# Layer-norm scaling as one VectorE operation per 128 rows, and new orders of work, in a macaron block of FFN, windowed attention and FFN

## The reference

```
def _layernorm(x, axis=-1, eps=1e-05):
    m = jnp.mean(x, axis=axis, keepdims=True)
    v = jnp.var(x, axis=axis, keepdims=True)
    return (x - m) / jnp.sqrt(v + eps)

x = x + 0.5 * ffn(_layernorm(x)); x = x + attn(_layernorm(x)); x = x + 0.5 * ffn(_layernorm(x))
```

```
shared = silu(X @ sW1 + sb1) @ sW2 + sb2
logits = einsum('btd,ed->bte', X, routing_W) + expert_bias
activation = sqrt(softplus(logits)); top_vals, top_idx = top_k(activation, 2)
routed = sum over e of combine[e] * (silu(X @ rW1[e] + rb1[e]) @ rW2[e] + rb2[e])
```

## Time and profile before

| quantity | value |
|---|---|
| median of 3 runs | 1796.23 us |
| the profiled execution | 1796.92 us |
| span of its instructions | 1795.2 us |
| PE busy | 1611.3 us (90%) |
| DVE busy | 1398.3 us (78%) |
| ACT busy | 1255.8 us (70%) |
| POOL busy | 991.3 us (55%) |
| PE's mean granted clock | 0.967 of full speed |

### The profile page before, as it was taken

One profiled execution on the slowest core, in us unless ns is written; L12 is line 12 of the kernel. 1 busy time (PEld: TensorE's weight loads), 2 busy tenths in 40 slices (PEclk: granted clock), 3 DMA queues, 4 the chain that ended last, 5 costly groups with the idle time before them and its releaser, 6 DMA issues.

```text
span 1795.2 us, 35300 instructions
## 1 busy us (share of the span) xinstructions
PE 1611.3 (90%) x10304; PEld 1412.1 (79%) x10304; DVE 1398.3 (78%) x4802; ACT 1255.8 (70%) x3656; POOL 991.3 (55%) x917
## 2 busy tenths in 40 slices
PE   1679899999999999999999999999999999998866
PEld 1557788888887888888787888888888888877755
DVE  4457688888879888888888888887988888785733
ACT  2247678687777768787777867787776868776732
POOL 1434465655566566656666565566656665653524
PEclk9979999999999999999999999999999999999878
DMA  3134443545453453535344353535345453534201
GB/s 90 55 113 115 130 122 108 143 121 145 123 143 92 122 150 114 144 115 153 112 123 123 108 144 117 149 121 144 97 114 156 113 143 116 157 96 133 75 24 59
DMA packets 286420, 211.94 MB, mean 118 GB/s; under 512 B 162666, under 2 KB 240900, under 8 KB 286228
## 3 DMA queue, kind: packets, MB, share of 16 engines
q1 hardware_dynamic: 282736, 209.57, 40.9%
q10 hardware_dynamic: 3460, 0.04, 0.1%
q0 software_dynamic: 32, 0.07, 0.0%
HBM read 146.06 MB, written 42.47 MB: 105 GB/s over the span
## 4 chain that ended last, share of the span: by engine, by line
PE 42%; DVE 19%; POOL 13%; issue 12%; ACT 9%; DMA 3%; SPq 3%; POOLq 0%; DVEq 0%; ACTq 0%
POOL zz L400 6%; PE gb L773 5%; PE gb L775 5%; PE gb L774 5%; PE yb L773 4%; PE yb L775 4%; PE yb L774 4%; PE ptb L832 3%; POOL gl L406 3%; PE sb_ L823 3%; POOL pr L384 2%; ACT xn L493 2%; DVE ag L725 2%; ACT pr L465 2%; DVE cfs L697 2%
## 5 line engine op out<-in xcount | busy, mean ns | idle before, releaser
L406 POOL TENSOR_TENSOR gl<-ag,gh 128x512 fp32r<-128x512 f32 x288 | 376.0, 1312 | 200.6 <-ACT gh L519 188.6
L384 POOL TENSOR_TENSOR pr<-pr,rinv 128x512 f32<-128x512 f32 x256 | 281.0, 1098 | 300.1 <-DVE rinv L667 299.9
L465 ACT ACTIVATE pr<-pr,mx 128x128 f32<-128x128 f32 x1024 | 397.0, 396 | 56.2 <-DVE mx L659 56.1
L773 PE MATMUL yb<-w2h,gh 128*128 128x256 f32 x1152 | 333.4, 289 | 6.2 <-POOL gl L406 6.2
L774 PE MATMUL yb<-w2h,gl 128*128 128x256 f32 x1152 | 322.2, 280 | 0.0
L775 PE MATMUL yb<-w2l,gh 128*128 128x256 f32 x1152 | 321.8, 279 | 0.0
L400 POOL TENSOR_TENSOR zz<-lp,phalf 128x8 f32<-128x8 f32 x128 | 220.0, 1734 | 117.1 <-DVE lp L622 117.1
L471 ACT ACTIVATE pth<-ptb 128x512 fp32r<-128x512 f32 x256 | 151.4, 591 | 173.8 <-PE cxb L775 95.0
L719 DVE SCALAR_TENSOR_TENSOR ag<-gb,b,gate 128x512 f32<-128x512 f32 x256 | 190.5, 744 | 92.1 <-ACT tt L525 66.7
L725 DVE SCALAR_TENSOR_TENSOR ag<-tt,ag 128x512 f32<-128x512 f32 x288 | 249.6, 867 | 3.1
L659 DVE CUSTOM_DVE_ANT_0 pr<-sb_,mask 128x128 f32<-128x128 f32 x1024 | 236.1, 286 | 14.6 <-issue 11.6
(11 more groups left out here) (144 smaller groups left out, 3577.9 us busy)
## 6 DMA issues: line engine op xcount, KB each, us to landing
gate<-gates_pair SPq DMA_DIRECT2D x256, 256.0 KB, 3.8
ks<-qk_dram SPq DMA_DIRECT2D x256, 128.0 KB, 3.0
qs<-qk_dram SPq DMA_DIRECT2D x512, 64.0 KB, 2.9
qk_dram<-qkh SPq DMA_DIRECT2D x64, 256.0 KB, 3.9
qk_dram<-qkl SPq DMA_DIRECT2D x64, 256.0 KB, 3.8
vb<-va SPq DMA_DIRECT2D x32, 384.0 KB, 6.8
xres<-L_attn_x_dram SPq DMA_DIRECT2D x16, 512.0 KB, 4.3
cx<-cd SPq DMA_DIRECT2D x512, 16.0 KB, 1.8
```

Of the source, the lines that this page charges most:

```text
L384: nc.gpsimd.tensor_tensor(pr[:, k], pr[:, k], rinv[:, k, :].unsqueeze(2).to_broadcast([P, NP, P]), ALU.mult).then_inc(a_pn, 1)
L406: nc.gpsimd.tensor_tensor(gl[:, k, :], ag[:, k, :], gh[:, k, :].bitcast(F32), ALU.subtract).then_inc(f_gl, 1)
L465: nc.scalar.activation(pr[:, k, r, :], pr[:, k, r, :], ACT.Exp, bias=mx[:, k, r:r + 1], scale=-1.0, accum_out=rsum[:, k, r:r + 1]).then_in ...
L773: nc.tensor.matmul(dst, ah, bh, start=start, stop=False, **kw)
```

## The change

The normalised rows are no longer made on ScalarE as x * rs + nb, but on VectorE as (x - mean) * rs, one `tensor_scalar` of 128x256 with two values per row. The four instructions of each `N2` step move from ScalarE to VectorE. GpSimd no longer computes nb, so `rstd` has two instructions where it had four, and the constant `mone` goes. The five orders are new, and the steps begin at another point of the pipeline.

```
-            def rstd(vals, r, neg, s, done):
+            def rstd(vals, r, s, done):
                 nc.gpsimd.tensor_tensor(r, vals[:, :, 1], epsb[:], ALU.add).then_inc(s, 1)
-                nc.gpsimd.tensor_tensor(neg, vals[:, :, 0], mone[:], ALU.mult).then_inc(s, 1)
-                pool.wait_ge(s, done + 2)
+                pool.wait_ge(s, done + 1)
                 nc.gpsimd.tensor_tensor(r, r, mhalf[:], ALU.pow).then_inc(s, 1)
-                pool.wait_ge(s, done + 3)
-                nc.gpsimd.tensor_tensor(neg, neg, r, ALU.mult).then_inc(s, 1)
...
-                    for t in range(NT):
-                        nc.scalar.activation(xn[:, t, :], src[:, t, :], ACT.Identity, bias=nb[:, t:t + 1],
-                                             scale=rs[:, t:t + 1]).then_inc(f_xn, 1)
...
+                elif s[1:] == "N2":
+                    n = nth(s, b)
+                    dve.wait_ge(f_rstd, 2 * n + 2)
+                    wait(dve, f_g1, 16 * n)
+                    wait(dve, a_xt, 2 * b if s[0] == "p" else 2 * min(b + 2, B))
+                    src = xin if s[0] == "p" else x2
+                    for t in range(NT):
+                        nc.vector.tensor_scalar(xn[:, t, :], src[:, t, :], mv[:, t, 0:1], rs[:, t:t + 1],
+                                                ALU.subtract, ALU.mult).then_inc(f_xn, 1)
```

`aN2` changes in the same way, with `mva` and `rsa`. Of the orders, one line of ScalarE's list (it shows `pt0` ahead of `pcr`, and no `N2`):

```
-cd14-1 pt0+1 ex1+0 cd15-1 pt1+1 ph0+0 qgh8-2 pct+1 pgh0+1 vh1+0 ex2+0 cd0+0 cth1-1 ph1+0 pt2+1 pgh1+1 ex3+0
+cd13-1 qgh7-2 pt0+1 pcr+1 ph15-1 cd14-1 ex0+0 pct+1 cd15-1 qgh8-2 ex1+0 pgh0+1 ph0+0 pt1+1 vh1+0 ex2+0 pt2+1
```

More of the change, by code:

```diff
@@ L19 @@
 ORDER_PE = """
[L20 to L24, removed]
@@ L25 @@
-S15+0 P13+0 qH8-1 qY5-1
+qH8-2 qY5-2 U13-1 P14-1 pH0+1 S0+0 pC+1 U14-1 P15-1 qY6-2 S1+0 pH1+1 U15-1 qY7-2 S2+0 P0+0 V1+0 qY8-2 pH2+1 U0+0
+P1+0 S3+0 pH3+1 pY0+1 S4+0 O0-1 O1-1 pH4+1 P2+0 U1+0 pY1+1 pH5+1 pY2+1 U2+0 qX0-1 qX1-1 S5+0 P3+0 pH6+1 qL-1
+pY3+1 pY4+1 S6+0 P4+0 U3+0 pH7+1 pH8+1 S7+0 P5+0 pY5+1 U4+0 pY6+1 qH0-1 S8+0 U5+0 qC-1 P6+0 pY7+1 pY8+1 qH1-1
+S9+0 U6+0 P7+0 qH2-1 S10+0 qY0-1 U7+0 P8+0 aX0+1 qH3-1 aX1+1 S11+0 qY1-1 U8+0 P9+0 Q00+1 qY2-1 Q01+1 U9+0 P10+0
+pX0+2 S12+0 pX1+2 qH4-1 qH5-1 pL+2 S13+0 P11+0 U10+0 qH6-1 Q10+1 Q11+1 qY3-1 S14+0 P12+0 U11+0 qH7-1 qY4-1 U12+0
@@ L26 @@
+P13+0 S15+0 V0+1
 """
 ORDER_ACT = """
-cd14-1 pt0+1 ex1+0 cd15-1 pt1+1 ph0+0 qgh8-2 pct+1 pgh0+1 vh1+0 ex2+0 cd0+0 cth1-1 ph1+0 pt2+1 pgh1+1 ex3+0
[L29 to L32, removed]
@@ L33 @@
-qgh4-1 ex13+0 qgh5-1 ph12+0 cd11+0 qh11+1 qt6-1 ex14+0 qt7-1 qgh6-1 cd12+0 ph13+0 vh0+1 ex15+0 qt8-1 ph14+0
-cd13+0 qgh7-1 pcr+2 ex0+1 ph15+0
+cth0-1 qt6-2 ex13-1 qh11+0 cd11-1 ph12-1 qgh5-2 ex14-1 cd12-1 qt7-2 vh0+0 ph13-1 qgh6-2 ex15-1 qt8-2 ph14-1
+cd13-1 qgh7-2 pt0+1 pcr+1 ph15-1 cd14-1 ex0+0 pct+1 cd15-1 qgh8-2 ex1+0 pgh0+1 ph0+0 pt1+1 vh1+0 ex2+0 pt2+1
+ph1+0 cth1-1 pgh1+1 pt3+1 ex3+0 cd0+0 pgh2+1 ph2+0 pt4+1 pgh3+1 cd1+0 pt5+1 ex4+0 cd2+0 qxh0-1 qxh1-1 pgh4+1
+ph3+0 pt6+1 ex5+0 pgh5+1 qen-1 pgh6+1 ph4+0 cd3+0 pt7+1 ex6+0 pt8+1 pgh7+1 cd4+0 ph5+0 pgh8+1 ex7+0 qt0-1 qcr-1
@@ L35 @@
+ph6+0 cd5+0 ex8+0 qgh0-1 qt1-1 qct-1 ph7+0 cd6+0 ex9+0 qt2-1 qgh1-1 ph8+0 cd7+0 axh0+1 axh1+1 qt3-1 qgh2-1
+ex10+0 cd8+0 qh00+1 ph9+0 ex11+0 qh01+1 pxh0+2 ph10+0 pxh1+2 cd9+0 qgh3-1 qt4-1 ex12+0 qt5-1 ph11+0 pen+2 cd10+0
+qgh4-1 qh10+1
 """
 ORDER_DVE = """
-ri15-1 mx0+0 pl14-1 qa8-2 mx1+0 ri0+0 pl15-1 pa0+1 qg8-2 ri1+0 pg0+1 mx2+0 pl0+0 vl1+0 pa1+1 pg1+1 qT-2 mx3+0
-pl1+0 pa2+1 ri2+0 pg2+1 aR0-1 pa3+1 aR1-1 qN1-1 ri3+0 pg3+1 pl2+0 mx4+0 pa4+1 pa5+1 pg4+1 qxl0-1 qxl1-1 mx5+0
-pg5+1 ri4+0 pl3+0 qLr-1 ri5+0 qLq-1 qR1-1 mx6+0 pl4+0 pa6+1 pg6+1 mx7+0 pa7+1 pl5+0 pg7+1 ri6+0 pa8+1 pg8+1
@@ L40 @@
[L40 to L43, removed]
+ri0+0 mx1+0 pa0+1 pg0+1 ri1+0 mx2+0 pl0+0 vl1+0 pa1+1 ri2+0 qT-2 pg1+1 pl1+0 mx3+0 pa2+1 pg2+1 pa3+1 aR0-1 pg3+1
+aR1-1 ri3+0 qN1-1 mx4+0 pl2+0 pa4+1 qN2-1 pg4+1 pa5+1 ri4+0 pg5+1 qxl0-1 qxl1-1 mx5+0 pl3+0 pa6+1 qLr-1 pg6+1
@@ L44 @@
+ri5+0 qLq-1 qR1-1 mx6+0 pl4+0 pa7+1 pg7+1 ri6+0 pa8+1 mx7+0 pg8+1 pl5+0 qR2-1 qa0-1 mx8+0 qg0-1 pl6+0 ri7+0 pT+1
+ri8+0 aN1+1 mx9+0 pl7+0 qa1-1 aN2+1 qg1-1 ri9+0 qa2-1 mx10+0 qg2-1 pl8+0 axl0+1 axl1+1 pN1+2 qa3-1 ri10+0 mx11+0
+pl9+0 pN2+2 ql00+1 ql01+1 qg3-1 ri11+0 pxl0+2 pxl1+2 mx12+0 pl10+0 qa4-1 qg4-1 ri12+0 pLr+2 qa5-1 pLq+2 mx13+0
+pl11+0 pR1+2 qa6-1 ri13+0 mx14+0 qg5-1 pl12+0 qg6-1 ql10+1 ql11+1 ri14+0 mx15+0 vl0+1 pl13+0 qa7-1 qg7-1 ri15+0
+pR2+2 pl14+0 mx0+1 qa8-1 pl15+0 qg8-1
 """
 ORDER_POOL = """
-pn11-1 qgl3-2 ctl0-1 pn12-1 qgl4-2 qgl5-2 pzz0+1 pn13-1 pzz1+1 pn14-1 pzz2+1 pzz3+1 qgl6-2 pn15-1 qgl7-2 pn0+0
@@ L47 @@
-pn1+0 qgl8-2 pgl0+1 ctl1-1 pgl1+1 pn2+0 pgl2+1 qrs-1 pn3+0 pgl3+1 pn4+0 pn5+0 pgl4+1 pgl5+1 qzz0-1 qzz1-1 qzz2-1
-pgl6+1 qzz3-1 pn6+0 pgl7+1 pgl8+1 pn7+0 qgl0-1 rsa+1 pn8+0 qgl1-1 prs+2 pn9+0 qgl2-1 pn10+0
+pn0+0 qgl8-2 pn1+0 pgl0+1 ctl0-1 ctl1-1 pgl1+1 pn2+0 pgl2+1 pn3+0 qrs-1 pgl3+1 pgl4+1 pn4+0 pgl5+1 pn5+0 pgl6+1
+qzz0-1 qzz1-1 qzz2-1 qzz3-1 pn6+0 pgl7+1 pgl8+1 pn7+0 qgl0-1 pn8+0 rsa+1 qgl1-1 pn9+0 qgl2-1 prs+2 pn10+0 pn11+0
+qgl3-1 pn12+0 qgl4-1 pzz0+2 pn13+0 pzz1+2 pzz2+2 qgl5-1 pzz3+2 pn14+0 pn15+0 qgl6-1 qgl7-1
@@ L350, in select @@
                 pool.wait_ge(w_const, done)
[L351 to L361, removed]
+            select(ident[:], ALU.not_equal, 1.0, 0, [[-1, P]], 1, 8)
+            select(mask[0:WIN, 0, :], ALU.is_ge, NEG, 0, [[-1, P]], 1, 9)
+            select(mask[0:WIN, 1, :], ALU.is_ge, NEG, -1, [[1, P]], -1, 10)
+            select(mask[0:WIN, 1, :], ALU.is_ge, NEG, WIN, [[-1, P]], 1, 11)
+            select(before[:], ALU.is_gt, 0.0, 0, [[1, E], [-1, E]], 0, 12)
+            select(rowlo[:, 0:1], ALU.is_ge, 0.0, -48, [[0, 1]], 1, 13)
+            select(rowlo[:, 0:1], ALU.is_ge, 0.0, 57, [[0, 1]], -1, 14)
+            select(rowlo[:, 0:1], ALU.not_equal, 0.0, -56, [[0, 1]], 1, 15)
             pool.dma_start(mask[WIN:2 * WIN, :, :], mask[0:WIN, :, :]).then_inc(w_mask, 16)
             pool.wait_ge(w_mask, 16)
-            def rstd(vals, r, neg, s, done):
+            def rstd(vals, r, s, done):
                 nc.gpsimd.tensor_tensor(r, vals[:, :, 1], epsb[:], ALU.add).then_inc(s, 1)
-                nc.gpsimd.tensor_tensor(neg, vals[:, :, 0], mone[:], ALU.mult).then_inc(s, 1)
-                pool.wait_ge(s, done + 2)
+                pool.wait_ge(s, done + 1)
                 nc.gpsimd.tensor_tensor(r, r, mhalf[:], ALU.pow).then_inc(s, 1)
-                pool.wait_ge(s, done + 3)
-                nc.gpsimd.tensor_tensor(neg, neg, r, ALU.mult).then_inc(s, 1)
             def step(s, b):
@@ L434, in step @@
             def step(s, b):
-                if s == "aN2":
-                    act.wait_ge(a_rstd, 4 * b + 4)
-                    act.wait_ge(f_g1, 16 * max(2 * b, 1))
-                    for t in range(NT):
-                        nc.scalar.activation(xn[:, t, :], x1[b % 2][:, t, :], ACT.Identity, bias=nba[:, t:t + 1],
-                                             scale=rsa[:, t:t + 1]).then_inc(a_xn, 1)
-                elif s[:3] == "axh":
+                if s[:3] == "axh":
                     c = int(s[3])
@@ L626, in step @@
                     dve.wait_ge(f_res, 2 * nth("p", b) + 2)
-                    wait(dve, a_rstd, 4 * b)
+                    wait(dve, a_rstd, 2 * b)
                     stats(x1[b % 2], stata, mva, a_stat, 8 * b)
+                elif s == "aN2":
+                    dve.wait_ge(a_rstd, 2 * b + 2)
+                    dve.wait_ge(f_g1, 16 * max(2 * b, 1))
+                    for t in range(NT):
+                        nc.vector.tensor_scalar(xn[:, t, :], x1[b % 2][:, t, :], mva[:, t, 0:1], rsa[:, t:t + 1],
+                                                ALU.subtract, ALU.mult).then_inc(a_xn, 1)
                 elif s[:3] == "axl":
@@ L679, in step @@
                         dve.wait_ge(a_x2, 2 * b + 2)
-                    wait(dve, f_rstd, 4 * n)
+                    wait(dve, f_rstd, 2 * n)
                     stats(xin if s[0] == "p" else x2, stat, mv, f_stat, 8 * n)
+                elif s[1:] == "N2":
[4 more added lines that the diff above has]
+                    src = xin if s[0] == "p" else x2
+                    for t in range(NT):
+                        nc.vector.tensor_scalar(xn[:, t, :], src[:, t, :], mv[:, t, 0:1], rs[:, t:t + 1],
+                                                ALU.subtract, ALU.mult).then_inc(f_xn, 1)
                 elif s[1:3] == "xl":
@@ L743, in _ @@
         def _(pe):
-            pe.wait_ge(w_const, 16)
+            pe.wait_ge(w_const, 15)
             pe.wait_ge(w_lo, NSPLIT + 2)
```

26 lines of the change are left out of this document (9 added, 17 removed).

## The result

The changed kernel takes 1806.73 us (median of 7 runs, 1803.74 to 1809.76) against 1796.23 us (7 runs, 1793.80 to 1799.24). The ratio is 1.0057, with a 95% interval of 1.0046 to 1.0069. It is slower by 10 us where 26 us faster was forecast. The profiled execution took 1807.23 us with a span of 1805.2 us.

The account below looks back on a forecast made before the run. TensorE's matmul stream was taken as the bound; 14 x (-1.0 router's chain, -0.6 small waits) = -22.4, ends -4, together -26 us on 1796.9, giving 1770 us; range 1735 to 1810, the forecast case's own 1760 to 1784.

Parts of the forecast that it names:

- small waits: PE's short waits before `S1`, `qX0` and `pX0`: expected to shrink by 0.6 us an iteration (0 to 0.64).
- The router's chain: Second FFN's router, from first logit instruction on DVE to `qC` on PE: 18.7 instead of 19.67 us, -1.0 an iteration.
- The powers: Four powers on POOL in the second FFN's router: 6.45 us instead of 8.13, as `pgl6` leaves them.
- no row says that a stall goes: Reason for taking only -1.0 us in the router; with the stalls of L606, L697 and L704 gone, -3.7.
- a stall or two leaves the router's chain: Rival: one DVE stall less per iteration gives 13 us more, two 25; 1745 to 1757 us, chance 0.18.
- PE's two waits: PE's waits before `S7` and `qC`, behind the second FFN's router: from 4.2 to 3.2 us an iteration.
- DVE's scalings: Twelve new `tensor_scalar` per iteration on DVE: 0.53 us each, 6.4 us in all (4.2 to 9.3), put at 0 cost.
- the stall of L605: DVE, router's ranks: 0.423 us, called the most a group shows on average; upper bound of one scaling 0.354 + 0.423.
- DVE's load: DVE's work per iteration: from 87.6 to 94.0 us (91.8 to 96.9), below the 102.5 us period, so covered.
- The slow rival: Throughout the loop DVE becomes the bound: 104.3 us an iteration, +21 us, 1817 us; chance 0.18.
- The ends: First transposes, batch 0's attention norm, last FFN's norm: each 1.1 us shorter, 3.3, plus 0.7 for start order; -4 us.
- The rule on what excludes what: On DVE and POOL: `tensor_scalar` and a GpSimd instruction can exclude each other, putting DVE's sum between middle and upper value.

## Why the prediction was wrong

**The step that failed is one that the prediction does not have.** Its sum counts DVE, ACT, POOL and PE, part by part, and nothing for SyncE. The other moves of the new orders went in as "small waits", -0.6 us. `OUT-2` behind `VS+0` stands in the diff of the lists, and the wait of `aR0` for the store is in the trace of before, at 3.2 us in 11 iterations. One such wait, 1.05 us, even stands in the row that gave the length of an iteration. The question to put to it was how far the store can be late. The answer was there: the store landed at 732.4 (728.77 + 3.6), 0.4 us before DVE was ready for `aR0` and 0.9 before it started at 733.27. In other iterations it took up to 5.1 us and `aR0` already waited. So nearly every microsecond more was going to hold DVE. Put right, this one word turns 1806.7 into 1770.9.

**How 3.84 us on DVE became 2.1 on PE, and more.** The late `aR0` delays `pl2` and the norm. PE's waits before `qX0` and `U2` are 1.3 and 0.8 us an iteration (14.4 and 9.2 us over about 11). In iterations without a fall of the clock PE stands idle for 4.1 to 5.0 us in all and they last about 102.4 us; with the store first it is 2.7 to 2.9, and they last 100.1. So the store took back what the change had won, 102.4 us being also the length before. The rest is the clock. In the window from 846 to 853 us, right behind the waits of an iteration, the granted clock is 0.76, a fall to the lower level of 1.2 GHz for about half of it, with PE busy throughout:

```profile
846.00:853.00 7.00, 7.00 (x44) 6.62 (x43) 5.69 (x21) 4.53 (x13) 2.28 (x2) 0.76 0.50 139
```

From 240 us to the last `S0` there are 7 such falls after and 6 before, but two of the 7 last twice as long: 30.7 us at the lower level against 20.5. They also cost more. Before, four of the six (at 1168.0, 1270.4, 1372.8 and 1475.2 us) come behind the wait for `S7`, with the one for `qC` still ahead, and that one shrinks from 2.0 to 0.1 us or less: the slow matmuls fill a wait, and the iteration is no longer than others. After, they come behind the waits for `qX0` or `qC`, and iterations with them last 104.4 to 106.4 us. With the store first there are six, 20.5 us again, and five of the six iterations with one last 101.4 to 101.7 us instead of 100.1. This is read from three traces and no experiment sets the clock, so it is argued and not shown.

**The router's chain** went the forecast way, and further. The logits on DVE start at 747.61 and `qC` is released at 765.52: 17.9 us, where 18.7 was forecast and 19.67 was before. The powers took the 6.45 us of the forecast within 0.1:

```profile
755.37 6.56 POOL L396 TENSOR_TENSOR zz<-lp,phalf 128x8 f32<-128x8 f32 x4 [1.48 <-DVE lp L603]
```

The 0.8 us more come from the ranks, where "no row says that a stall goes". Two went (1.69 us), and two smaller ones came in the softplus. DVE's timeline of the ranks, before and after:

```profile
748.55 1.15 DVE L604 TENSOR_TENSOR xn<-lg 128x256 f32<-128x256 f32 x1
749.73 1.39 DVE L605 TENSOR_TENSOR xn<-xn,before 128x256 f32<-128x256 f32 x1
```

```profile
749.41 0.42 DVE L585 TENSOR_TENSOR xn<-lg 128x256 f32<-128x256 f32 x1
749.87 0.42 DVE L586 TENSOR_TENSOR xn<-xn,before 128x256 f32<-128x256 f32 x1
750.33 1.40 DVE L587 TENSOR_TENSOR xn<-xn 128x256 f32<-128x256 f32 x1
```

Before, a `pr` and two `gl` of POOL in a row lay beside them; now POOL starts its `gl` only at 749.92. That is 1.69 us less, of which `pg6` and the new stalls of 0.66 and 0.27 us in the softplus take a part. It is the rival "a stall or two leaves the router's chain", which was given 1745 to 1757. PE's two waits sum to 2.4 us on average over iterations 3 to 11 (1.8 and 0.6) against 4.2, where 3.2 was forecast.

**DVE's scalings.** 0.53 us each was forecast, between 0.354 and 0.777. They take 434 ns on average, 5.2 us for twelve (461 and 5.5 with the store first); the two groups of the changed kernel over the span are (min, median, max in ns, and the mean in the last row):

```profile
L676 DVE TENSOR_SCALAR xn<-xres,mv,rs x128: 399/405/1294, 34.3 to 1749.4; 128x256 f32<-128x256 f32 x128
```

```profile
L614 DVE TENSOR_SCALAR xn<-xres,mva,rsa 128x256 f32<-128x256 f32 x64 | 22.0, 407 | 1.4 <-POOL rsa L369 1.4
```

The forecast of a median of 354 was wrong: with two values per row it is 405. Wrong too is that 0.423 us, the stall of L605, is "the most a group shows on average": L697 stalls by 0.83 in a mean of 1020 ns. DVE's load was put at 94.0 us of an iteration and is 88.8 with the store first (975.12 us of 1100, at 100.2), against 87.1 before (935.14 of 1100, at 102.5). The scalings do add their 5.5, but `ag` (L725, now L721) falls from 867 to 780 ns on average, and other stalls go as well. Covered the scalings are, in the new lists: the kernel with the store first has them all and runs at the forecast time. The slow rival, DVE as the bound, is out. Slower came by another way, and none of the rivals held it.

**The ends.** The norm is shorter by 1.0 to 1.1 us at all three places, as forecast: PE's first transposes start at 35.84 instead of 36.83, its wait before the transposes of batch 0's attention norm is 6.02 instead of 7.14 us, and that before the last FFN's is 5.42 instead of 6.54. But the whole of the ends, put at -4, agrees only by luck: ahead of `S0` of batch 1 and behind that of batch 15 it is -4.1 us in the changed kernel (-0.3 and -3.8), and -0.7 with the store first (+2.4 and -3.1). What takes the rest is open. **The small waits** of PE before `S1` (0.3 us), `pX0` and `S11` (0.1 each) did go, 0.5 us where I took 0.6; the 0.34 before `pX0` was the weight load's wait (PEld), not PE's 0.13. `pC` takes 0.2 to 0.3 back.

So the forecast of 1770 was right for the change without its one move of a store, and its number by luck in part: with the store first the steady part is 25.9 us shorter, where the sum had 22.4, and the ends 0.7, where it had 4. In the steady part an iteration without a fall of the clock takes 100.1 us, where 100.9 was forecast, and the falls, which cost little before, take some of that back.

The rule on what excludes what, from the Trainium skill ("SBUF — State Buffer", "Who interferes with whom"), agrees in kind here. A `tensor_scalar` does wait for a `gl`: in the kernel with the store first, DVE's four scalings at 731.03 take 2.26 us where four of 0.405 would take 1.6, and POOL's `gl` lies beside them. It cost little, as only 14 of 192 were caught in this kernel and 15 in the changed one.

```profile
731.03 2.26 DVE L676 TENSOR_SCALAR xn<-xres,mv,rs 128x256 f32<-128x256 f32 x4
```

```profile
730.88 1.29 POOL L402 TENSOR_TENSOR gl<-ag,gh 128x512 fp32r<-128x512 f32 x1 [0.52 <-ACT gh L500]
```
